# A twelve-sublayer decoder on one core: values between queries and keys, third parts on DVE, later loads between stores

## What is computed

```python
for lvl in range(LEVELS):
    x = query[:, ::2 ** lvl, :]
    outs.append(_mha(x, in_proj_w[lvl], in_proj_b[lvl], out_w[lvl], out_b[lvl]))
...
qkv = x @ w_in.T + b_in
q, k, v = jnp.split(qkv, 3, axis=-1)
```

## Time and profile before

| | us |
|---|---|
| median of 3 runs (4989.38 to 4997.85) | 4994.53 |
| time of the profiled execution | 4987.66 |
| its span | 4985.9 |
| TensorE busy in it | 4178.0 (84%) |
| DVE busy | 2851.3 (57%) |
| ACT busy | 2371.4 (48%) |
| GpSimd busy | 1485.7 (30%) |

### The profile page before, as it was taken

One profiled execution on the slowest core, in us unless ns is written; L12 is line 12 of the kernel. 1 busy time (PEld: TensorE's weight loads), 2 busy tenths in 40 slices (PEclk: granted clock), 3 DMA queues, 4 the chain that ended last, 5 costly groups with the idle time before them and its releaser, 6 DMA issues. The chain is left out here.

```text
span 4985.9 us, 69673 instructions
## 1 busy us (share of the span) xinstructions
PE 4178.0 (84%) x20292; PEld 1974.0 (40%) x20292; DVE 2851.3 (57%) x6426; ACT 2371.4 (48%) x4593; POOL 1485.7 (30%) x1306
## 2 busy tenths in 40 slices
PE   8779756689778996897979799999997988189986
PEld 5322345377542332573334233333335644012223
DVE  3448473401667884104860388778863265298866
ACT  4437331243233775233753354545551255269993
POOL 3112141212130111112120288778881223200111
PEclk9669977699887998897989899999998999579998
DMA  7545212354033332674333311221210043623321
GB/s 258 131 100 126 47 48 34 122 201 146 33 136 58 62 62 65 229 243 141 79 82 146 126 60 61 68 68 60 64 39 37 31 119 85 197 61 91 95 54 37
DMA packets 330787, 486.64 MB, mean 98 GB/s; under 512 B 84916, under 2 KB 232996, under 8 KB 315732
## 3 DMA queue, kind: packets, MB, share of 16 engines
q1 hardware_dynamic: 323744, 449.92, 31.4%
q0 software_dynamic: 6384, 32.61, 2.1%
q10 hardware_dynamic: 348, 0.44, 0.0%
HBM read 325.01 MB, written 143.92 MB: 94 GB/s over the span
## 5 line engine op out<-in xcount | busy, mean ns | idle before, releaser
L1307 POOL TENSOR_TENSOR lc_totals<-lc_totals,lc_weights 128x1024 f32<-128x1024 f32 (+1 forms) x320 | 623.3, 1948 | 164.9 <-DVE lc_totals L1256 134.4
L1216 ACT ACTIVATE lc_weights<-ps 128x1024 f32<-128x1024 f32 x384 | 393.5, 1025 | 441.3 <-PE ps L1133 428.2
L1237 DVE TENSOR_REDUCE lc_part_max<-ps 128x2 f32<-128x1024 f32 x384 | 466.4, 1214 | 199.8 <-PE ps L1113 198.3
L1133 PE MATMUL ps<-lc_q,lc_k 64*128 64x512 f32 x1536 | 396.8, 595 | 0.0
L1143 PE MATMUL ps<-lc_weights,lc_v 128*64 128x512 f32 x1536 | 372.0, 605 | 0.0
L828 DVE TENSOR_REDUCE l1x_core_part_max<-ps 128x1 f32<-128x512 f32 x512 | 316.6, 683 | 72.0 <-PE ps L652 71.9
L787 ACT ACTIVATE l3x_core_weights<-ps 128x512 f32<-128x512 f32 x512 | 334.2, 711 | 6.6 <-PE ps L720 6.3
L824 DVE CUSTOM_DVE_ANT_0 l3x_core_unused<-ps,l3x_core_mask_q 128x512 f32<-128x512 f32 x512 | 330.4, 686 | 4.6 <-DVE l3x_core_row_max L832 3.4
L787 ACT ACTIVATE l1x_core_weights<-ps 128x512 f32<-128x512 f32 x512 | 266.2, 602 | 84.3 <-PE ps L720 84.1
L770 ACT ACTIVATE ps<-l3x_core_mask_k 128x512 f32<-128x512 f32 x384 | 277.0, 722 | 31.4 <-DMA l3x_core_mask_k<-in_mask_k 31.4
L652 PE MATMUL ps<-l3x_core_k,l3x_core_q 96*128 96x512 bf16 x512 | 213.9, 419 | 53.3 <-DVE l3x_core_part_max L824 38.8
(11 more groups left out here) (474 smaller groups left out, 8621.0 us busy)
## 6 DMA issues: line engine op xcount, KB each, us to landing
cf_w<-in_L1f_w SPq DMA_DIRECT2D x32, 1024.0 KB, 7.6
lc_k<-latent_k SPq DMA_DIRECT2D x32, 768.0 KB, 6.5
lc_v<-latent_values SPq DMA_DIRECT2D x32, 768.0 KB, 5.0
latent_k<-feed_staged SPq DMA_DIRECT2D x64, 256.0 KB
latent_values<-feed_staged SPq DMA_DIRECT2D x64, 256.0 KB
k_heads<-proj_parts SPq DMA_DIRECT2D x40, 384.0 KB, 2.6
q_heads<-proj_parts SPq DMA_DIRECT2D x32, 384.0 KB, 2.6
q_heads<-proj_parts SPq DMA_DIRECT2D x32, 256.0 KB, 3.0
```

Of the source, the lines that this page charges most:

```text
L1133: mm = nc.tensor.matmul(out[j], k_tile[g % RING][strip(j), i * P:(i + 1) * P], q_tile[g % RING][strip(j), :], start=False, stop=True)
L1216: nc.scalar.activation(weights[:, i % TILES, :, :], k.ps[:, B0 + (i % 2) * HEADS:B0 + (i % 2 + 1) * HEADS, 0:nq], ACT.Exp, scale=scale).th ...
L1237: nc.vector.reduce_max(own, k.ps[:, A0:A0 + HEADS, :], AX).then_inc(a_taken, 1)
L1307: nc.gpsimd.tensor_tensor(total, total, own, ALU.add).then_inc(added_by_pool, 1)
```

## The change

1. `spread_among(some, others, last)` puts the members of one list evenly between those of another, and the last few at the end. In the pyramid values now lie between the fine keys, and coarse values between the coarse queries and keys, two of them at the end. In l1x the kept units lie between the keys, in l2a and l3a between queries and keys, four at the end.
2. DVE makes the third part itself (`take_low`): for unit i - 1 after the subtraction of unit i. GpSimd has nothing left in the stage.
3. SyncE issues the loads of `prefetch` evenly among the stores. Loads of `late` get a third member, `every`: 0 means at the start as before, else load p is issued ahead of unit `every * (p + 1)`. Only the three coarse weights have a number, 2. X is loaded in four pieces.

```diff
-            for (_, pairs), landed in zip(late, late_in):
-                for tile, source in pairs:
-                    sync.dma_start(tile, source).then_inc(landed, 16)
-            for tile, source in prefetch:
-                sync.dma_start(tile, source).then_inc(prefetched, 16)
+
+            def load_late(unit):
+                for (_, pairs, every), landed in zip(late, late_in):
+                    for p, (tile, source) in enumerate(pairs):
+                        if every * (p + 1) == unit:
+                            sync.dma_start(tile, source).then_inc(landed, 16)
+
+            load_late(0)
...
             for n, unit in enumerate(units):
+                if n:
+                    load_late(n)
+                for tile, source in islice(later, len(prefetch) * (n + 1) // len(units) - len(prefetch) * n // len(units)):
+                    sync.dma_start(tile, source).then_inc(prefetched, 16)
...
+            def take_low(i):
+                width = units[splits[i]][2]
+                dve.wait_ge(middle, i + 1)
+                nc.vector.tensor_tensor(parts[:, i % 3, 2, 0:width], rest[:, i % 2, 0:width],
+                                        parts[:, i % 3, 1, 0:width], ALU.subtract).then_inc(low, 1)
...
                 nc.vector.tensor_tensor(rest[:, i % 2, 0:width], whole, parts[:, i % 3, 0, 0:width], ALU.subtract).then_inc(remainder, 1)
-
-        @block.gpsimd
-        def _(pool):
-            for i, n in enumerate(splits):
-                width = units[n][2]
-                pool.wait_ge(middle, i + 1)
-                nc.gpsimd.tensor_tensor(parts[:, i % 3, 2, 0:width], rest[:, i % 2, 0:width],
-                                        parts[:, i % 3, 1, 0:width], ALU.subtract).then_inc(low, 1)
+                if i:
+                    take_low(i - 1)
+            if splits:
+                take_low(len(splits) - 1)
...
+def spread_among(some, others, last):
+
+    out, taken = [], 0
+    for n, unit in enumerate(some):
+        out.append(unit)
+        upto = (len(others) - last) * (n + 1) // len(some)
+        out += others[taken:upto]
+        taken = upto
+    return out + others[taken:]
...
+            units = queries + spread_among(keys, value_units(lambda c, t: k.xT[:, c, t * P:(t + 1) * P], P, w[:, 0, :, 2 * C:], values), 0)
...
+            units += spread_among(coarse_operands, coarse_values, 2)
...
-                              (fine_units, [(w[:, lvl], inp["L0_in_w"][lvl]) for lvl in levels])],
+                              (fine_units, [(w[:, lvl], inp["L0_in_w"][lvl]) for lvl in levels], CH)],
...
+            project_stage(k, queries + spread_among(keys, others, 4) if late else spread_among(queries + keys, others, 4), [], ahead=True,
+                          late=late, prefetch=prefetch)
...
-                       (k.head_cols[:], inp["head_cols"]), (k.X[:], inp["x"])]
+                       (k.head_cols[:], inp["head_cols"])]
+        k.constants += [(k.X[:, t:t + HG, :], inp["x"][:, t:t + HG, :]) for t in range(0, NT, HG)]
```

More of the change, by code:

```diff
@@ L17 @@
 import math
+from itertools import islice
 from contextlib import ExitStack, contextmanager
@@ L126, in project_stage @@
         parts_stored, others_stored, value_stored, late_in = stored[0:3], stored[3], stored[4:4 + VALUES], stored[4 + VALUES:]
-        late_of = {unit: i for i, (unit, _) in enumerate(late)}
+        late_of = {unit: i for i, (unit, *_) in enumerate(late)}
         @block.sync
@@ L1566, in pyramid_attention @@
         with nc.sbuf_tensor("pyr_wqkv", [P, 4, CH, 3 * C], F32) as w, nc.sbuf_tensor("pyr_zeros", [P, H * QUAD], F32) as zeros:
-            units = []
-            for store, col in ((q_parts, 0), (k_parts, C)):
-                units += split_units(lambda c, t: k.xT[:, c, t * BANK:(t + 1) * BANK], BANK, w[:, 0, :, col:col + C], bias[:, 0, col // P:col // P + CH], store)
-            units += value_units(lambda c, t: k.xT[:, c, t * P:(t + 1) * P], P, w[:, 0, :, 2 * C:], values)
+            queries, keys = (split_units(lambda c, t: k.xT[:, c, t * BANK:(t + 1) * BANK], BANK, w[:, 0, :, col:col + C],
+                                         bias[:, 0, col // P:col // P + CH], store) for store, col in ((q_parts, 0), (k_parts, C)))
+            units = queries + spread_among(keys, value_units(lambda c, t: k.xT[:, c, t * P:(t + 1) * P], P, w[:, 0, :, 2 * C:], values), 0)
             fine_units = len(units)
+            coarse_operands, coarse_values = [], []
             levels = (1, 2, 3)
@@ L1579, in pyramid_attention @@
             for store, col in ((q_coarse, 0), (k_coarse, C)):
-                units += [("split", [(cols[lvl], w[:, lvl, c, col + m * P:col + (m + 1) * P], tokens(lvl, c, b), c == 0, c == CH - 1)
+                coarse_operands += [("split", [(cols[lvl], w[:, lvl, c, col + m * P:col + (m + 1) * P], tokens(lvl, c, b), c == 0, c == CH - 1)
                                      for lvl in levels for c in range(CH)], S,
@@ L1591, in pyramid_attention @@
                 tiles = [v_coarse[b * 4 + place[lvl] // P + i, 0:n, :] for b in range(B) for i in range((S >> lvl) // n)]
-                units += value_units(rows, n, w[:, lvl, :, 2 * C:], tiles)
+                coarse_values += value_units(rows, n, w[:, lvl, :, 2 * C:], tiles)
+            units += spread_among(coarse_operands, coarse_values, 2)
             def batch(b):
@@ L1598, in pyramid_attention @@
                           [(v_coarse[b * 4 + 3, S >> 3:P, :], zeros[S >> 3:P, :]) for b in range(B)],
-                          late=[(CH * b, batch(b)) for b in range(1, B)] + [
-                              (CH * B, [(w[:, 0, :, C:3 * C], inp["L0_in_w"][0, :, :, C:3 * C])]),
-                              (fine_units, [(w[:, lvl], inp["L0_in_w"][lvl]) for lvl in levels])],
+                          late=[(CH * b, batch(b), 0) for b in range(1, B)] + [
+                              (CH * B, [(w[:, 0, :, C:3 * C], inp["L0_in_w"][0, :, :, C:3 * C])], 0),
+                              (fine_units, [(w[:, lvl], inp["L0_in_w"][lvl]) for lvl in levels], CH)],
                           prefetch=k.constants + prefetch, fills=[(k.ones[:], 1.0), (zeros[:], 0.0)])
@@ L1652, in self_or_cross_attention @@
                 source = ctxT
-                late = [(T // BANK * CH, [(ctxT[:], inp["ctxT"])])]
+                late = [(T // BANK * CH, [(ctxT[:], inp["ctxT"])], 0)]
             if b_name:
                 prefetch.append((vb[:], inp[v_b]))
-            project_stage(
-                k, split_units(lambda c, t: k.xT[:, c, t * BANK:(t + 1) * BANK], BANK, w[:, :, 0:C],
-                               bias[:, 0:CH] if b_name else None, q_parts)
-                + split_units(lambda c, t: source[:, c, t * BANK:(t + 1) * BANK], BANK, w[:, :, C:2 * C],
-                              bias[:, CH:] if b_name else None, k_parts)
-                + kept_units(lambda c, t: source[:, c, t * P:(t + 1) * P], w[:, :, 2 * C:], values), [], ahead=True,
-                late=late, prefetch=prefetch)
+            queries = split_units(lambda c, t: k.xT[:, c, t * BANK:(t + 1) * BANK], BANK, w[:, :, 0:C],
+                                  bias[:, 0:CH] if b_name else None, q_parts)
+            keys = split_units(lambda c, t: source[:, c, t * BANK:(t + 1) * BANK], BANK, w[:, :, C:2 * C],
+                               bias[:, CH:] if b_name else None, k_parts)
+            others = kept_units(lambda c, t: source[:, c, t * P:(t + 1) * P], w[:, :, 2 * C:], values)
+            project_stage(k, queries + spread_among(keys, others, 4) if late else spread_among(queries + keys, others, 4), [], ahead=True,
+                          late=late, prefetch=prefetch)
         dense_att = k.xT
```

3 lines of the change are left out of this document (2 added, 1 removed).

## The result

The changed kernel took **4965.14 us** (median of 5 runs, 4961.27 to 4966.27) against 4994.53 in the runs beside it: ratio 0.9941, 95% interval 0.9926 to 0.9955. That is 29 us less where 38.6 were forecast; 4965 lies inside the range of 4942 to 4980. The profiled execution took 4962.08 with a span of 4960.3, 25.6 less than the profiled one of before.

A forecast was written before the change was run, and what follows sets the result against it. The ring of three part buffers was taken as the bound. Pyramid 18.4, l1x 10.5, l2a and l3a 2.5 each and l3x 4.7 sum to 38.6 us less: profiled 4949.1, median 4956; range 4942 to 4980.

The forecast's parts named there:

- The ring of three buffers: Part buffers waiting for stores set the splits' pace: in l1x 2.32 us per unit against TensorE's 1.71.
- Third part 0.69: The third part's subtraction, moved to DVE, takes 0.69 us, as a same-size subtraction free of GpSimd's work.
- Rival B: The third part on DVE costs 1.45 us, as under GpSimd's work; 11 us gained in all, 4983; chance 0.06.
- Fourth cast 19.6: Pyramid: with loads moved from the head, DVE's fourth cast comes near 19.6 us instead of 33.91.
- key's chain 2.9: ACT and DVE's serial chain with values between keys: cast, subtraction, middle part, value, next evacuation, 2.9 us per key.
- Pyramid, 18.4 forecast: Stage of 116.0 us against 134.4: TensorE through at 110.2, waits of 1.5 included, then 2.8 and 3.0 of tail.
- l1x, 10.5 forecast: l1x's stage ends at 1499.1 to 1499.4 against 1509.9, with TensorE through at 1497.9.
- 15 steps of about 2.47: l2a and l3a: steps from first to last of 16 split casts, reaching 41.3 us; stage 47.3 against 49.8.
- l3x, 4.7 forecast: Third part on DVE saves 0.38 us in each of 10.5 pairs and 0.7 at the end.
- Rival A: The new chain of ACT and DVE holds TensorE: only 20 us gained in all, 4974; chance 0.17.
- C: Pyramid: loads between stores delay stores behind them, deciding from 6.5 us landings; 14 us slower, 5008; chance 0.05.
- The DMA rule: Batch transfers to at least 1 MiB; X's four 512 KB loads take 12.8 us against 6.8, unread in the stage.

The follow-up runs named there:

- run 9: The kernel before with four part buffers instead of three, nothing else changed: ratio 0.9904 to the kernel before.
- run 6: The changed kernel with the prefetches spread over all units but the last 12: ratio 0.9941 to the kernel before.
- run 4: The changed kernel with the third part back on GpSimd, order and loads kept as changed: ratio 0.9965 to the kernel before.
- run 10: The changed kernel with X loaded again in one piece of 2 MB: ratio 0.9940 to the kernel before.
- runs 6 and 8: The changed kernel with prefetches done before the last 12 units: alone 0.9941; with four part buffers too, 0.9870 (4921.82 us).

## Why the prediction was right, and where it was off

- **What bounds the five stages.** "The ring of three buffers is the bound" was right, and the prediction didn't follow it to its end: a fourth buffer in the kernel before gives 47.5 us (run 9), the change 29. Most of what the three edits win is won around that one number; with four buffers 11 us of it are left.
- **Third part 0.69.** Measured 0.685; no cast over 0.43. Rival B is out.
- **Fourth cast 19.6, l1x's queries 5.23 for two, l3x's pairs 4.9, key's chain 2.9.** Measured 19.72, 5.3, 4.89, 2.77. The model of the turn holds where landings were taken from the same stage.
- **Pyramid, 18.4 forecast, 14.1 measured: two terms mis-sized.** Landings were taken from l1x (3.40); beside the loads they are 1.0 to 1.6 us longer, so two queries take 6.3 to 6.8 us. Two of the prediction's own signs of being wrong came with it: stores that land later than 4 us, and TensorE idle on evacuations among the keys, once for over 1 us (1.13). It cost little, two stops of 1.94 us where 1.5 was added for waits. TensorE ends at 112.4 instead of 110.2; the other 1.8 us are many small ones in the first run and the coarse levels. The tail was put at 5.8 us and is 7.9. The last third part came as forecast, 0.9 us behind TensorE's end (1.1), but the issues behind it take 0.5 to 0.9 us each and go on to 117.7, not to 113.0. Taking the two prefetches out of them (run 6) did not shorten the tail.
- **l1x, 10.5 forecast, 8.8 measured.** TensorE ends 76.0 us after its start instead of 74.6, the tail is 1.9 instead of 1.5.
- **l2a and l3a, 2.5 each forecast.** l3a gives 2.2, l2a loses 1.1. The first eight matmuls of l2a ran slow and those of l3a did not:

```profile
2266.04 6.53 PE L187 MATMUL ps<-xT,ahead 128*128 128x512 f32 x8 [0.73 <-PEq L1372]
...
3943.68 3.67 PE L187 MATMUL ps<-xT,ahead 128*128 128x512 f32 x8 [0.73 <-PEq L1372]
```

In the kernel before both ran slow. The first 6 us of l2a and l3a there, and of l2a and l3a in the changed kernel (columns as in the earlier trace rows, the clock is the third number from the end):

```profile
2293.00:2299.00 6.00, 6.00 (x9) 2.66 (x10) 1.12 (x2) 0.63 (x2) 0.00 (x0) 0.62 0.18 66
3970.50:3976.50 6.00, 6.00 (x11) 2.75 (x12) 1.22 (x3) 1.51 (x3) 0.00 (x0) 0.75 0.30 66
...
2266.00:2272.00 6.00, 5.96 (x8) 2.54 (x9) 1.12 (x2) 0.60 (x1) 0.00 (x0) 0.52 0.00 0
3943.70:3949.70 6.00, 6.00 (x16) 3.09 (x17) 2.68 (x5) 2.58 (x5) 0.00 (x0) 1.00 0.00 0
```

So l2a's first cast comes 4.42 us after its start in both kernels, and the clock doesn't explain its 1.1 us, which is no more than one stage is sure to (48.7 to 51.0 in the kernels with the new order and three buffers, 49.9 before). l3a's first cast comes 2.71 us after its start where it was 4.22: 1.5 of its 2.2 us are the clock's, and luck. The term that was mis-sized is "15 steps of about 2.47": they are 2.59 in l2a and 2.58 in l3a, 1.9 and 1.6 us in all. In l2a the end is 1.7 us longer as well, 7.7 from the last cast where 6.0 was forecast, 1.4 of it the prefetch that lands last. In l3a the fast start pays for the slower steps, which is why 47.3 forecast and 47.6 measured lie so near.

- **l3x, 4.7 forecast, 3.5 measured.** The pairs came as said; the end did not gain the 0.7. SyncE issues a prefetch between the last two stores there; without it (run 6) the stage is 0.9 us shorter, which one profile can't tell from chance.
- **Rival A** (ACT and DVE's chain of keys holds TensorE) did not come beyond the two stops above, but the chain is in the tails of l2a and l3a: in l3a TensorE is through with the last key at 3980.9, and it is cast at 3985.02. In l1x the last key is cast 0.8 us after TensorE has made it, with GpSimd's third part (run 4) 3.7 after. **C** did not come: the queries' landings of 4.4 to 5.0 us lie below its point of 6.5.
- **The DMA rule weighed.** X in four pieces lands 7.0 us each, and in one piece it gives the same time (run 10). By the fit of the Trainium skill (DMA: Bandwidth & Descriptors, Anatomy of one DMA — SWDGE (gpsimd) path) a load of 512 KB takes 3.2 us, an estimate. That fit is for a DMA issued from GpSimd, and these loads are issued by SyncE, among stores that are on their way too. The trace's 7.0 is more than twice the estimate, and the measurement decides.
- **The sum.** No stage gave more than was forecast; together they gave 27.5 us of 38.6, so the forecast median of 4956 is 9 us too low.

What stays open: what would shorten the pyramid's tail of 7 to 8 us, how much the early prefetches of runs 6 and 8 give, and what decides the clock at which a stage starts.

## What to carry to other kernels

When an engine waits for a store in a ring of buffers, try one more buffer before moving work around: in l3x a turn of 4.9 us was shared by two units with three buffers and by three with four, and one run with one more buffer gave 47.5 us where all the moves together gave 29. Where work is moved onto another engine, ask what covers it: with all values last the same subtraction on DVE cost 9 us, with values between the keys it gained 9 to 12, and there its place in DVE's list made no difference that could be measured. Before a stage's gain or loss is put down to a change, compare the clock at its start in both profiles. Units of another kind placed between fill an engine's waits, but they shorten how far ahead a fixed number of banks reaches and uncover the tail that they had covered at the end.

## What the runs showed of the hardware

- DVE's cast takes 0.41 to 0.43 us alone and up to 1.35 when it starts while a GpSimd subtraction of 1.16 is under way. In run 4's lines the GpSimd one ends at 1455.51 + 1.16 = 1456.67 and the cast that started at 1456.31 ends at 1456.94, 0.27 later. The Trainium skill (SBUF — State Buffer, SBUF: two separate sides) says that the two engines share a port pair that one of them holds for its whole instruction; the trace agrees.
- A store's landing is not a price of its own: for l3x's queries it is 3.1 us with three buffers, 7.5 with four (and 7.6 in run 9), 4.6 with five, while the stage gets shorter each time.
- After a stop of 6.08 us TensorE's next four matmuls ran at the lower clock (2.07 us for 1.03, granted clock 0.50), so that stop cost more than its own length. After stops of 0.81 and 1.13 us it took 1.98 us for what else takes 1.88.
- The first eight matmuls of l2a took 5.06 to 6.71 us over the fourteen profiles and those of l3a 3.67 or 5.16 to 5.37. Two profiles of one stage can so differ by 1.7 us for that reason alone.
